# Attention, adapter and feed-forward kernel on one core: GpSimd's indirect transfers tied to TensorE's progress, loads around the hand-over reordered

## The chip, the core and the metric

One core of a Trainium2 chip runs one program. The metric is the device time in microseconds (us) of one execution, lower is better. The profile shows one execution; its span runs from the first to the last instruction.

## The reference

x holds 128 batches of 32 tokens with 512 features, all in float32. What is computed, in order:

- style: every batch picks one of 16 matrices of 32 x 32 by its style id, and its 32 tokens are mixed by it (`einsum('bct,bcd->bdt')`).
- attention on that: q, k, v by w_qkv, clipped to +-8; layer norm of q and k with their weights; 32 heads of 16 features, 32 keys each, bias by distance, causal mask, softmax, output projection; the result is added to x (x1).
- adapter: every batch picks one of 8 matrices of 512 x 512 by its adapter id: y = x1 times that matrix.
- feed-forward on y: relu(y up)^2 down (inner size 1024), plus a routed part, y fc1 expert fc2 scaled per token by the sum of the two largest of 8 gate logits; then layer norm with gamma and beta. Result: x1 plus that.

## The kernel before, in words

The host sorts nothing: the kernel ranks the batches by adapter id itself, makes tables of row numbers, and works on the 4096 tokens as 32 tiles (T) of 128 tokens, 4 batches each, in that order. The large products are exact to nearly float32: each operand is split into a high and a low part, and three products are added (hi x hi, hi x lo, lo x hi). So a projection of one tile is 12 matmuls of 128x128 by 512 columns (L555). ACT makes the high parts, DVE or GpSimd the low ones.

fc1, expert and fc2 are multiplied once at the start: `latent` (L653) and `make_route(c)` (L664, four blocks of four matmuls, c = 0 to 3), copied out of PSUM by ACT (`keep_route`) and stored to HBM by SP's queue.

**Attention** is a software pipeline of 32 rounds, i = 0 to 31, one iteration of a loop written out for each engine. In round i TensorE does, in this order: style of tile i+1 (L545, 8 matmuls); projection of q of tile i; first half of the values of tile i-4 (L573, 48 small matmuls); projection of k; second half of the values; turn_slot (L630); projection of v; the turn of tile i-4's values (L585); the turn of q of tile i-1 (L603); adapt_slot (L644, 12 matmuls); the turn of k; first half of the scores of tile i-2 (L618, 48 small matmuls of 64x32 by 128 columns); the output projection of tile i-4 (L595, 12 matmuls); second half of the scores. ACT scales and rounds q and k, takes the exponential, and copies results out of PSUM; DVE adds bias and takes the row maximum (L1186, L1190), makes low parts, clips, divides, adds x.

GpSimd's round: style_bd for tile i+2 (L1458), scatter_slot of slot i-7 (L1491: rows of y to HBM by an index table), subtract_max of tile i-3 (L1520), low part of the adapter weights (L1526), gather_x and gather_style of tile i+3 (L1470, L1474), low_probs of tile i-3 (L1532), gather_slot of slot i-5 (L1485: rows of x1 back from HBM), the small steps of the layer norm to shift (L1555 to L1565), low part of v (L1569). A slot is up to four batches of one adapter; slots run LAG = 6 rounds behind the tiles. All of these indirect DMAs are issued by GpSimd, which the trace shows busy for about 1 us with each.

The keys and values of four batches are spread into block form (kx, vx) by small copies from SBUF to SBUF on SP's queue (`spread_k` L468, `spread_v` L477, four of 64 or 68 KB each). SP's queue is one list: x1 stores, spreads, weight chunks, y rows (load_y), adapter weights (load_w2, 1 MB each), each behind the waits of what stands before it. In rounds 4 to 23 the feed-forward weights are also split in 20 chunks and the parts stored to HBM; ACT's queue fetches them back later (`fetch`).

**Hand-over.** From round 31 on, the last tiles' attention and the first group's feed-forward are interleaved by hand: turns of y (L681), up(0, f) (L718, 12 matmuls each), scores, values, output projections.

**Feed-forward**: 8 groups of 512 tokens; each has up (8 x 12 matmuls), gates, and four down stages (L735, L742), then normalization on DVE, and a scatter of 128 result rows by GpSimd (`store`, L1498). The remaining slots of the adapter run inside.

The order before, in GpSimd's loop:

```python
                if i > LAG:
                    scatter_slot(i - LAG - 1)
                if live(i - 3):
                    subtract_max(i - 3)
                ...
                if live(i + 3):
                    gather_x(i + 3)
                    gather_style(i + 3)
                if live(i - 3):
                    low_probs(i - 3)
                if i >= LAG - 1:
                    gather_slot(i - LAG + 1)
```

`upto(e, "s", t)` waits until the scores of tile t are done, `upto(e, "o", t)` until its values are; `kx`, `qhi`, `cv` and so on are counted the same way.

## Time and profile before

| | |
|---|---|
| median of 3 runs | 1190.45 us (1190.12 to 1190.9) |
| profiled execution | 1192.36 us, its span 1190.6 us |
| TensorE matmuls | busy 1137.5 us, 96% of the span |
| weight loads (beside the matmuls) | 902.8 us, 76% |
| DVE, ACT, GpSimd | 638.6, 555.7, 705.0 us |
| granted TensorE clock, mean | 0.99 of full speed |
| moved between HBM and core | 98.16 MB read, 38.27 MB written |

PE is TensorE's matmuls, PEld its weight loads, POOL is GpSimd, SP the sync engine; a q behind the name (SPq) is the engine's queue that issues DMAs. A group of instructions shows its start, how long it lasts, the line of the kernel and what it writes and reads; in brackets the idle time of the engine before it and who ended it. "issue" means that the engine waited for nothing that the profile shows. A granted clock of 1.00 is the 2.4 GHz level, 0.50 the 1.2 GHz level.

### The profile page before, as it was taken

How to read it: one execution, taken by the hardware profiler on the slowest of the kernel's cores; microseconds unless marked ns; L12 is line 12 of the kernel's file. 1: busy time of each engine (PE TensorE's matmuls, PEld its weight loads, DVE VectorE, ACT ScalarE, POOL GpSimd, SP SyncE). 2: the span in 40 equal slices, each digit the busy share in tenths (PEclk: the TensorE clock that was granted, in tenths of full speed). 3: DMA queues.
4: the chain of work that ended last, by engine and by line, in shares of the span. 5: the costliest groups of instructions: out<-in, count | busy, mean ns of one | idle time of the engine just before them, and what ended most of it. 6: DMA issues, size and time to landing. Idle time of an engine off the chain costs nothing.

```text
span 1190.6 us, 27392 instructions
## 1 busy us (share of the span) xinstructions
PE 1137.5 (96%) x11124; PEld 902.8 (76%) x11124; DVE 638.6 (54%) x1042; ACT 555.7 (47%) x915; POOL 705.0 (59%) x610
## 2 busy tenths in 40 slices
PE   6999999999999999999997999999999999999994
PEld 4777777777777777777776778787888878787883
DVE  5567575656566666656555344444444444443432
ACT  4365666666666657565655432415142332313120
POOL 4366778787778787878673545545545445433332
PEclk9999999999999999999998999999999999999998
DMA  7124555455554545344455743142413212120101
GB/s 272 45 66 158 176 173 168 170 174 178 154 187 151 193 154 194 118 155 149 142 176 201 251 148 97 62 136 69 137 63 100 82 53 89 54 89 15 56 18 44
DMA packets 60172, 152.38 MB, mean 128 GB/s; under 512 B 11280, under 2 KB 12048, under 8 KB 54672
## 3 DMA queue, kind: packets, MB, share of 16 engines
q1 hardware_dynamic: 42576, 106.06, 26.7%
q0 software_dynamic: 12224, 34.10, 9.0%
q10 hardware_dynamic: 5248, 10.49, 2.5%
q8 instruction: 89, 1.46, 0.5%
q14 instruction: 35, 0.29, 0.1%
HBM read 98.16 MB, written 38.27 MB: 115 GB/s over the span
## 4 chain that ended last, share of the span: by engine, by line
PE 93%; DMA 2%; issue 2%; DVE 1%; ACT 1%; POOL 0%; SPq 0%; ACTq 0%; DVEq 0%
PE bank L555 23%; PE pair L742 15%; PE bank L718 14%; PE bank L644 9%; PE bank L595 8%; PE bank L735 7%; PE pair L618 3%; PE bank L545 3%; PE pair L573 3%; PE bank L603 2%; PE bank L630 2%; PE bank L585 1%; PE bank L691 1%; PE bank L681 1%; DMA kx<-k_hl 1%
## 5 line engine op out<-in xcount | busy, mean ns | idle before, releaser
L1526 POOL TENSOR_TENSOR w_lo<-w2t,w_hi 128x2048 fp32r<-128x2048 f32 x38 | 175.8, 4626 | 13.0 <-ACT w_hi L902 13.0
L555 PE MATMUL bank<-wqkv_hi,h_hi 128*128 128x512 f32 x384 | 159.5, 415 | 3.5 <-ACT q_hi L1000 1.9
L555 PE MATMUL bank<-wqkv_hi,h_lo 128*128 128x512 f32 x384 | 151.5, 395 | 0.5 <-issue 0.5
L555 PE MATMUL bank<-wqkv_lo,h_hi 128*128 128x512 f32 x384 | 150.4, 392 | 0.0
L1578 POOL TENSOR_TENSOR u_lo<-act,u_hi 128x512 fp32r<-128x512 f32 x64 | 82.5, 1290 | 106.5 <-ACT u_hi L1072 106.3
L1613 POOL TENSOR_SCALAR fve<-fmv 128x1 f32<-128x1 f32 x32 | 24.7, 772 | 153.6 <-DVE fmv L1438 153.6
L1520 POOL TENSOR_TENSOR probs<-probs,row_max 128x1024 f32<-128x1024 f32 x32 | 61.1, 1910 | 89.6 <-DVE row_max L1190 89.5
L718 PE MATMUL bank<-yT_hi,up_hi 128*128 128x512 f32 x256 | 103.4, 404 | 0.0
L742 PE MATMUL pair<-down_hi,u_hi 128*128 128x512 f32 x256 | 100.9, 394 | 0.0
L742 PE MATMUL pair<-down_hi,u_lo 128*128 128x512 f32 x256 | 100.8, 394 | 0.0
L718 PE MATMUL bank<-yT_hi,up_lo 128*128 128x512 f32 x256 | 100.6, 393 | 0.0
L718 PE MATMUL bank<-yT_lo,up_hi 128*128 128x512 f32 x256 | 100.3, 392 | 0.0
L742 PE MATMUL pair<-down_lo,u_hi 128*128 128x512 f32 x256 | 100.3, 392 | 0.0
L1383 DVE TENSOR_TENSOR act<-act 128x512 f32<-128x512 f32 x59 | 48.8, 827 | 95.6 <-ACT act L1068 95.6
L555 PEld LDWEIGHTS bank<-wqkv_hi,h_hi 128*128 128x128 f32 x384 | 72.6, 189 | 18.8 <-issue 4.2
L902 ACT ACTIVATE w_hi<-w2t 128x2048 fp32r<-128x2048 f32 x38 | 72.7, 1914 | 30.2 <-DMA w2t<-in_w 30.2
L1433 DVE TENSOR_TENSOR total<-total,pair 128x512 f32<-128x512 f32 x32 | 22.0, 688 | 119.9 <-PE pair L742 119.9
L1068 ACT ACTIVATE act<-bank 128x512 f32<-128x512 f32 x64 | 38.3, 598 | 102.2 <-PE bank L718 102.0
L555 PEld LDWEIGHTS bank<-wqkv_hi,h_lo 128*128 128x128 f32 x384 | 72.5, 189 | 17.7 <-issue 0.9
L1158 ACT ACTIVATE total<-bank,weight 128x512 f32<-128x512 f32 x32 | 22.0, 688 | 131.5 <-PE bank L735 131.5
L555 PEld LDWEIGHTS bank<-wqkv_lo,h_hi 128*128 128x128 f32 x384 | 72.7, 189 | 13.7 <-issue 0.8
L1532 POOL TENSOR_TENSOR p_lo<-probsT,p_hi 128x1024 bf16<-128x1024 f32 x32 | 69.1, 2158 | 23.3 <-ACT p_hi L945 22.8
(175 smaller groups left out, 2915.8 us busy)
## 6 DMA issues: line engine op xcount, KB each, us to landing
w2t<-in_w SPq DMA_DIRECT2D x38, 1024.0 KB
vx<-v_hl SPq DMA_DIRECT2D x128, 68.0 KB
x_rows<-x1t SPq DMA_DIRECT2D x32, 256.0 KB, 4.6
x1g<-x_rows SPq DMA_DIRECT2D x32, 256.0 KB, 3.4
kx<-k_hl SPq DMA_DIRECT2D x124, 64.0 KB
yt<-y_rows SPq DMA_DIRECT2D x7, 1024.0 KB, 6.7
ffn_high<-w_high SPq DMA_DIRECT2D x20, 256.0 KB, 4.2
ffn_low<-w_low SPq DMA_DIRECT2D x20, 256.0 KB, 4.5
```

Of the source, the lines that this page charges most:

```text
L555: m = e.matmul(into, a[:, c, :], b[:, n, c, :], start=(c == 0 and k == 0), stop=(c == KC - 1 and k == 2))
L595: m = e.matmul(B6, a[:, j, :], b[:, j, :], start=(j == 0 and k == 0), stop=(j == BPT - 1 and k == 2))
L644: m = e.matmul(into, a[:, P * c:P * c + P], b[:, c, :], start=(c == 0 and k == 0), stop=(c == KC - 1 and k == 2))
L718: i = e.matmul((B2, B3)[n % 2], a[:, w, cols], b[m % 2][:, c, :], start=(c == 0 and k == 0), stop=(c == KC - 1 and k == 2))
L735: i = e.matmul((B6, B7)[n % 2], a[m % 2][:, c, toks], b[:, c, :], start=(c == 0 and k == 0), stop=(c == KC - 1 and k == 2))
L742: i = e.matmul(pair[:, n % 2, :], a[f][:, toks], b[:, f, :], start=(f == 0 and k == 0), stop=(f == FC - 1 and k == 2))
L902: e.activation(w2_hi[:, :, :], w2t[:, :, :], ACT.Copy).then_inc(d_whi, 1)
L1383: e.tensor_tensor(act[n % 2][:, :], act[n % 2][:, :], act[n % 2][:, :], ALU.mult) \
L1520: e.tensor_tensor(probs[:, :, :], probs[:, :, :], row_max[:, :].rearrange("p (h o) -> p h o", o=1) .broadcast_to([P, HEADS, SEQ]), ALU.sub ...
L1526: e.tensor_tensor(w2_lo[:, :, :], w2t[:, :, :], w2_hi[:, :, :].bitcast(F32), ALU.subtract).then_inc(d_wlo, 1)
L1532: e.tensor_tensor(p_lo[:, :], probsT[:, :], p_hi[:, :], ALU.subtract).then_inc(A["plo"], 1)
L1578: e.tensor_tensor(u_lo[n % FC][:, :], act[n % 2][:, :], u_hi[n % FC][:, :].bitcast(F32), ALU.subtract) \
```

## The change

- GpSimd: scatter_slot waits for the scores of tile i-3 (for the last slot, tile T-3); gather_x and gather_style wait for the values of tile i-4; gather_slot stands ahead of low_probs. In the start the style rows of tile 0 are gathered before its x rows, with semaphores of their own, and gather_x(1) comes behind the first style. In the down stages the store of the tile before is issued ahead of the wait for the statistics.
- Start: the ids are the first loads of SP's queue; the second part of the constants is loaded by ACT's queue. Only make_route(0) stays ahead of round 0; make_route(1), (2), (3), their copies and stores move to rounds 2, 3, 4 (and one round later for the stores), into another bank.
- Keys of tiles 0 to 2 are turned in bank B4 instead of B5, without the wait for DVE's clip of v; ACT rounds q and k of tile 0 at the end of round 1 instead of at the start of round 2.
- Hand-over: the up weights are fetched in two sets, the even chunks (2 MB) in round 31 where all (4 MB) were, the odd ones (2 MB) after high_probs(T-3); up(0,4) waits for those. y of group 1 and the adapter weights of slot_up(0) are loaded behind the v spread of tile T-2 and the x1 store of T-4; the last v spread moves ahead of the x1 store of tile T-3.

```diff
--- before
+++ after
@@ -323,6 +323,7 @@
     a_x = [sem(f"a_load{i}") for i in range(XR)]
+    a_rows = [sem(f"a_rows{i}") for i in range(XR)]
     a_store = [sem(f"a_store{i}") for i in range(2)]
@@ -349,7 +350,8 @@
     m_gate, m_ghi, m_glo = sem("m_gate"), sem("m_ghi"), sem("m_glo")
-    m_up, m_route, m_down = sem("m_up"), sem("m_route"), sem("m_down")
+    m_up = [sem("m_up_low"), sem("m_up_high")]
+    m_route, m_down = sem("m_route"), sem("m_down")
     d_zero, d_w2, d_x = sem("d_zero"), sem("d_w2"), [sem("d_x0"), sem("d_x1")]
@@ -380,6 +382,12 @@
+    def k_bank(t):
+        return B4 if t < 3 else B5
+
+    def route_bank(c):
+        return pair[:, 0, :] if c == 0 else B6
+
     def last_slot(m):
@@ -388,7 +396,6 @@
-            e.dma_start(cst[:, C_WMASK:C_SIZE], consts[:, C_WMASK:C_SIZE]).then_inc(s_cst, 16)
             for dst, src in ((ids_row[:, :], adapter_ids.broadcast_to([P, BATCHES])),
@@ -401,17 +408,18 @@
             load_stage(1)
-            e.wait_ge(a_x[0], 32)
+            e.wait_ge(a_x[0], 16)
             load_stage(2)
...
             load_stage(3)
-            for c in range(KC):
+            def store_route(c):
                 e.wait_ge(s_routec, c + 1)
                 e.dma_start(route_rows[:, c, :], route_f[c][:, :]).then_inc(s_kept, 16)
+
+            store_route(0)
             e.dma_start(gate_raw[:, :, :], gate).then_inc(m_gate, 16)
             e.wait_ge(s_tables, 2)
-            e.wait_ge(s_route, KC)
@@ -488,15 +496,15 @@
                     spread_k(i - 2)
+                if i in (3, 4, 5):
+                    store_route(i - 2)
                 if 0 <= i - 4 < CHUNKS:
...
                     load_y(0)
-                if i == T - 1:
-                    load_y(1)
-                if i >= LAG - 1:
+                if LAG - 1 <= i < T - 1:
                     load_w2(i - LAG + 1)
@@ -507,8 +515,10 @@
             store_x1(T - 4)
+            load_w2(slot_up(0))
+            load_y(1)
+            spread_v(T - 1)
             store_x1(T - 3)
-            spread_v(T - 1)
@@ -536,7 +546,7 @@
-                e.wait_ge(a_x[t % XR], 32 * (t // XR + 1))
+                e.wait_ge(a_x[t % XR], 16 * (t // XR + 1))
                 upto(e, "style", t)
@@ -588,7 +598,9 @@
                 upto(e, "olo", t)
-                e.wait_ge(s_wlo, 4)
+                if t == 0:
+                    e.wait_ge(s_wlo, 4)
+                    e.wait_ge(s_routec, KC)
                 upto(e, "x1", t - 1)
@@ -659,9 +671,9 @@
                 if c >= 2:
-                    e.wait_ge(s_routec, c - 1)
+                    e.wait_ge(s_routec, c)
                 for k in range(LC):
-                    m = e.matmul(pair[:, c % 2, :], latT[:, k, P * c:P * c + P], fc2_sb[:, k, :],
+                    m = e.matmul(route_bank(c), latT[:, k, P * c:P * c + P], fc2_sb[:, k, :],
                                  start=(k == 0), stop=(k == LC - 1))
@@ -704,9 +716,11 @@
                 if n == 0:
-                    e.wait_ge(m_up, 64)
+                    e.wait_ge(m_up[0], 64)
                     upto(e, "khi", T - 1)
                     upto(e, "klo", T - 1)
+                if n == KC:
+                    e.wait_ge(m_up[1], 32)
                 if n >= 2:
@@ -753,7 +767,6 @@
             e.matmul(B4[:, 0:1], after[:, :], first[:, :], start=True, stop=True).then_inc(s_tp, 1)
-            make_route(0)
             style(0)
@@ -761,7 +774,7 @@
                 .then_inc(s_tp, 1)
-            make_route(1)
+            make_route(0)
             for i in range(T):
@@ -773,8 +786,9 @@
                 if i == 0:
-                    make_route(2)
                     style(1)
+                if i in (2, 3, 4):
+                    make_route(i - 1)
                 if live(i - 4):
@@ -782,8 +796,6 @@
                     project(i, 1, B3, "pk")
-                if i == 0:
-                    make_route(3)
                 if live(i - 4):
@@ -803,8 +815,9 @@
                 if live(i - 1):
-                    upto(e, "cv", i)
-                    turn_qk(i - 1, kn[(i - 1) % 2], "kn", B5, "tk")
+                    if i > 3:
+                        upto(e, "cv", i)
+                    turn_qk(i - 1, kn[(i - 1) % 2], "kn", k_bank(i - 1), "tk")
                 if live(i - 2):
@@ -920,6 +933,12 @@
+            def fetch_up(ready, part, first_, last_):
+
+                dst = (up_hi, up_lo)[part][:, first_:last_:2, :]
+                e.dma_start(dst.bitcast(F32), ffn_parts[part][first_:last_:2].rearrange("c p n -> p c n")) \
+                    .then_inc(ready, 16)
+
             def high_y(m, c):
@@ -968,16 +987,16 @@
                 e.wait_ge(s_route, c + 1)
-                e.activation(route_f[c][:, :], pair[:, c % 2, :], ACT.Copy).then_inc(s_routec, 1)
-
+                e.activation(route_f[c][:, :], route_bank(c), ACT.Copy).then_inc(s_routec, 1)
+
+            e.dma_start(cst[:, C_WMASK:C_SIZE], consts[:, C_WMASK:C_SIZE]).then_inc(s_cst, 16)
             high_weights(0)
...
                 keep_lat(n)
+            high_h(0)
             high_weights(1)
             keep_route(0)
-            high_h(0)
             high_weights(2)
-            keep_route(1)
             e.wait_ge(s_qkln, 16)
@@ -1010,16 +1029,15 @@
                 live = lambda t: 0 <= t < T
-                if live(i - 2):
+                if i >= 3:
                     high_q(i - 2, B3)
-                    high_k(i - 2, B5, k_hl)
-                if i == 0:
-                    keep_route(2)
+                    high_k(i - 2, k_bank(i - 2), k_hl)
                 if live(i + 1):
...
                     high_weights(3)
-                    keep_route(3)
+                if i in (2, 3, 4):
+                    keep_route(i - 1)
                 if i == 2:
@@ -1030,16 +1048,16 @@
                     upto(e, "pq", T - 1)
-                    fetch(m_up, up_hi[:, 0:4, :], 0, 0, 4)
-                    fetch(m_up, up_lo[:, 0:4, :], 1, 0, 4)
+                    fetch_up(m_up[0], 0, 0, 4)
+                    fetch_up(m_up[0], 1, 0, 4)
                 if live(i - 3):
...
                     upto(e, "pk", T - 1)
-                    fetch(m_up, up_hi[:, 4:8, :], 0, 4, 4)
-                    fetch(m_up, up_lo[:, 4:8, :], 1, 4, 4)
+                    fetch_up(m_up[0], 0, 4, 8)
+                    fetch_up(m_up[0], 1, 4, 8)
                 if live(i - 4):
@@ -1050,7 +1068,10 @@
                     scale_q(i - 1, B3)
-                    scale_k(i - 1, B5)
+                    scale_k(i - 1, k_bank(i - 1))
+                if i == 1:
+                    high_q(0, B3)
+                    high_k(0, k_bank(0), k_hl)
                 if i >= LAG:
@@ -1088,6 +1109,8 @@
             high_probs(T - 3)
+            fetch_up(m_up[1], 0, 1, 8)
+            fetch_up(m_up[1], 1, 1, 8)
             relu(0)
@@ -1336,7 +1359,7 @@
                     low_q(i - 2, B3)
-                    low_k(i - 2, B5, k_hl)
+                    low_k(i - 2, k_bank(i - 2), k_hl)
                 upto(e, "pq", t)
@@ -1454,7 +1477,7 @@
                 upto(e, "h", t - 2)
-                e.wait_ge(a_x[t % XR], 32 * (t // XR + 1))
+                e.wait_ge(a_rows[t % XR], 16 * (t // XR + 1))
                 e.tensor_tensor(style_bd[t % 2][:, :, :],
@@ -1472,7 +1495,7 @@
                 e.indirect_dma_start(out=style_rows[t % XR][:, :], out_offset=None, in_=style_w,
-                                     in_offset=rows(style_idx, t)).then_inc(a_x[t % XR], 16)
+                                     in_offset=rows(style_idx, t)).then_inc(a_rows[t % XR], 16)
@@ -1506,11 +1529,11 @@
             e.wait_ge(s_tables, 1)
+            gather_style(0)
             gather_x(0)
-            gather_style(0)
-            gather_x(1)
             e.wait_ge(s_cst, 16)
             style(0)
+            gather_x(1)
             gather_style(1)
@@ -1537,6 +1560,7 @@
                 if i > LAG:
+                    upto(e, "s", i - 3)
                     scatter_slot(i - LAG - 1)
@@ -1545,12 +1569,13 @@
                 if live(i + 3):
+                    upto(e, "o", i - 4)
                     gather_x(i + 3)
                     gather_style(i + 3)
+                if i >= LAG - 1:
+                    gather_slot(i - LAG + 1)
                 if live(i - 3):
                     low_probs(i - 3)
-                if i >= LAG - 1:
-                    gather_slot(i - LAG + 1)
                 upto(e, "aggr", t)
@@ -1578,6 +1603,7 @@
+            upto(e, "s", T - 3)
             scatter_slot(LAST)
@@ -1609,14 +1635,14 @@
                     n = GROUP * m + t
+                    if n:
+                        store(n - 1)
                     e.wait_ge(S["aggr"], n + 1)
...
                         .then_inc(S["rstd"], 1)
-                    if n:
-                        store(n - 1)
                     if t == 1:
...
                             scatter_slot(slot_down(m))
```

## Rows read from the trace of the kernel before

**Rows 1.** The page, part 4: the chain that ended last, by engine.
```profile
PE 93%; DMA 2%; issue 2%; DVE 1%; ACT 1%; POOL 0%; SPq 0%; ACTq 0%; DVEq 0%
```

**Rows 2.** TensorE's waits: us in total, times, longest us.
```profile
PE pair L618 <- issue: 10.2, 30, 0.5
...
PE pair L618 <- DMA kx<-k_hl: 5.3, 1, 5.3
...
PE bank L555 <- ACT q_hi L1000: 1.9, 1, 1.9
...
PE bank L644 <- DVE xgT_lo L1179: 1.5, 1, 1.5
PE bank L603 <- DVE vf L1168: 1.0, 3, 0.3
```

**Rows 3.** Windows over 54 score halves: from:to length, busy and count by engine.
```profile
127.04:128.41 1.37, 0.86 (x48) 0.60 (x48) 1.00 0.91 298
...
446.68:447.21 0.53, 0.53 (x48) 0.46 (x48) 1.00 0.12 39
...
sum 48.68, PE 37.99 PEld 28.36; mean PE 0.70 PEld 0.53
```

**Rows 4.** One round: start us, us, engine, line, operation [idle before <-releaser].
```profile
429.27 0.47 POOL L1458 TENSOR_TENSOR style_bd<-style_rows,cst 128x128 f32<-128x128 f32 x1
...
429.91 1.10 POOL L1491 DMA_INDIRECT y_rows<-ys,slot_rows  x1 [0.17 <-issue]
...
430.63 0.68 DVE L1220 TENSOR_TENSOR x1t<-bank,xt 128x512 f32<-128x512 f32 x1
...
431.19 0.25 PE L618 MATMUL pair<-kx,q_hi 64*32 64x128 bf16 x4 [0.29 <-issue]
...
434.14 1.91 POOL L1520 TENSOR_TENSOR probs<-probs,row_max 128x1024 f32<-128x1024 f32 x1 [3.13 <-DVE row_max L1190]
...
439.26 0.66 PE L630 MATMUL bank<-cst,xg 128*128 128x128 f32 x4
...
440.79 1.01 POOL L1470 DMA_INDIRECT xt<-in_x,tile_rows  x1 [0.16 <-issue]
...
445.39 1.03 POOL L1485 DMA_INDIRECT xg<-x_rows,slot_rows  x1 [0.16 <-issue]
```

**Rows 5.** Windows over values halves (two together, one clean), timeline at 78.
```profile
sum 2.98, PE 1.76 PEld 1.20; mean PE 0.88 PEld 0.60
...
111.42:111.98 0.56, 0.56 (x48) 0.45 (x48) 1.00 0.02 7
...
78.04 0.39 PE L555 MATMUL bank<-wqkv_hi,h_hi 128*128 128x512 f32 x1 [0.49 <-issue]
```

**Rows 6.** Timeline of the start; window with its granted clock (0.50).
```profile
18.92 1.98 PE L664 MATMUL pair<-fc_sb,latT 128*128 128x512 f32 x4
...
27.04 0.46 POOL L1458 TENSOR_TENSOR style_bd<-style_rows,cst 128x128 f32<-128x128 f32 x1 [3.78 <-DMA style_rows<-in_style_w,style_idx]
...
50.56:53.97 3.41, 3.41 (x9) 2.65 (x8) 0.61 (x2) 0.00 (x0) 0.00 (x0) 0.50 0.23 81
```

**Rows 7.** The hand-over: window (clock, DMA share, GB/s last), timeline, page part 6.
```profile
628.00:634.00 6.00, 4.04 (x125) 3.59 (x120) 5.05 (x8) 4.57 (x11) 1.90 (x1) 1.00 1.05 405
...
633.49 0.22 PE L573 MATMUL pair<-vx,p_lo 128*32 128x68 bf16 x4 [1.68 <-issue]
...
636.61 1.25 DVE L1224 TENSOR_TENSOR yT_lo<-bank,yT_hi 128x512 fp32r<-128x512 f32 x2
...
641.22 0.77 PE L718 MATMUL bank<-yT_hi,up_hi 128*128 128x512 f32 x1
...
x1g<-x_rows SPq DMA_DIRECT2D x32, 256.0 KB, 3.4
```

**Rows 8.** Timeline of the end.
```profile
1178.49 0.75 DVE L1447 SCALAR_TENSOR_TENSOR ot<-total,frstd,x1g 128x512 f32<-128x512 f32 x1 [0.94 <-POOL frstd L1616]
1179.88 0.96 POOL L1498 DMA_INDIRECT out<-ot,tile_rows  x1 [0.30 <-issue]
```

## The prediction, made before the changed kernel ran

> **What bounds the kernel now.** I read the page's chain first: TensorE carries 93% of it [rows 1]. So no other engine has to get faster; what can be won is time in which TensorE stands. Next come the waits of TensorE, longest in total first [rows 2]. The largest is no wait for a result: 10.2 us before score matmuls, in 30 pieces of at most 0.5 us, put down to "issue". Then 5.3 us once, for a copy into kx; 1.9 us once, for q_hi; 1.0 us in three waits for DVE's clip of v. The adapter's matmuls (L644, 456 of them) have one wait, for DVE, and none on issue.
>
> The third reading is of single score halves: 48 small matmuls each, from their first matmul to the first of the next group [rows 3]. A clean half takes 0.53 us, the one at 127.04 took 1.37. From round 5 to round 31 there are 54 halves with 48.68 us in all, so 48.68 - 54 x 0.53 = 20.1 us are lost in them; 20 of the 54 are clean. The fourth is the timeline of one round [rows 4]. GpSimd issues its scatter from 429.91 to 431.01; the second score half began at 430.33, issued 44 of its 48 matmuls, stood for half a microsecond and finished with four at 431.19. In the round after, the slot gather runs from 445.39 to 446.42 and the first half starts at 446.68: clean. Where that gather comes 0.3 us later, the first half is hit too. Each of the 34 slow halves has an indirect DMA of GpSimd over it, none of the 20 clean ones has. Two halves of values in rounds 4 and 5 lie under gathers as well: 2.98 us for both, where a clean one takes 0.56 (row of 111.42) [rows 5].
>
> **Scatter and slot gather (the main term).** Scatter s now waits for the scores of that round's end, so its 1.10 us start behind them, at some 431.0 instead of 429.91, under style's eight matmuls and the first project. It costs GpSimd nothing: it idles 3.13 us before subtract_max [rows 4], which waits for the row maximum, itself later than the scores; 1.1 us of scatter fit. What is queued behind it (subtract_max, low_w2) keeps its time. The gathers wait for values of four tiles back, over at 439.26 in that round; GpSimd reaches gather_x only at 440.79 [rows 4], 1.5 us later, so this wait never ends last in the steady rounds. The slot gather goes ahead of low_probs: 443.2 to 444.2, 2.4 us before the scores; low_probs shifts by 1.1 us to 446.4, and values need it 9 us later. The instructions behind them (var_eps to shift) stay. GpSimd's round then ends with style_bd at 429.74, 1.1 us before the earlier end of the scores. In rounds with a weight chunk DVE's add of x ends only at 431.31 [rows 4], so the maximum moves forward by 0.1 of the 0.5 us; the project that needs the low part of q, made after it, still starts 0.8 us behind it, so TensorE is not held. I take the whole 20.1 us; the low end is 7, where each of the 26 scatters costs a 0.5 us stall in its new place.
>
> **Values in rounds 4 and 5.** 2.98 - 2 x 0.56 = **1.9 us**; gathers wait until values are over. Low_probs comes up to 2 us later, needed a round later.
>
> **Start.** Ids go first and the other constants by ACT's queue: SP spends some 0.47 us on each issue, so ids leave and land 0.45 us earlier. Four route blocks of 1.9 to 2.0 us each (18.92 is one; back to back 1.4 to 1.8 us) [rows 6] stood ahead of and between the first projects; one stays, three move to rounds 2, 3 and 4. That frees 5.0 us at the start. But tile 2's style rows, issued by 20.60, landed only just before 27.04 (GpSimd waited 3.78 us for them) [rows 6]: the weight loads share the transfer. So data cap what TensorE can gain. Tile 1's rows are now asked for 0.5 us later, behind GpSimd's first style_bd; by tile 2's delay I put their landing near 23.3 us. With style, project of k and project of v from there, round 1 starts 2.9 us earlier (ends: 0, if the landings rule, and 5.0). The three blocks cost 5.0 again in rounds 2 to 4. What they fill: the 1.9 us wait for q_hi, which also goes because ACT rounds q of tile 0 before it waits for the statistics, and 0.8 us before project in round 3 (low part of q). With the 1.9 us wait goes what followed it: from 50.56 to 53.97 the granted clock was 0.50, the 1.2 GHz level [rows 6], 3.4 us for 1.7 us of work. Turning k into bank 4 for the first three tiles drops the 1.0 us on DVE's v [rows 2]. Start: 2.9 - 5.0 + 1.9 + 1.7 + 0.8 + 1.0 = **3.3 us**, ends 0.4 and 5.4.
>
> **Hand-over from attention (round 31 on).** Here TensorE stood 1.68 us inside values and 5.30 us until kx landed [rows 7]; the DMA engines were full (share 1.05, 405 GB/s) with four 1 MB loads of up weights, 1 MB of y and 1 MB of adapter weights. Two of the four, y and the adapter now go behind the spreads. SP's queue reaches the k spread at 628.6 as before, its four issues end at 631.0, and by the 3.4 us from issue to landing that the median load of x1g takes [rows 7], an upper bound for a copy a quarter as large, kx is there by 634.4. That doesn't give 6 us: up(0,0) needs the low parts of all four turned y chunks, and DVE made the last at 636.61 to 637.86, behind a transpose that waits for ACT's exp, a chain from the scores at 628 with no DMA in it. Up(0,0) started at 641.22 and can start at 637.7: **3.5 us**. What is late next is that low part. The clock had fallen to the 1.2 GHz level (0.77 us for the matmul at 641.22, where the one at 78.04 took 0.39) [rows 5, 7]; TensorE will still stand some 1 to 2.4 us at two places here, so I count nothing back; the high end, clock held and y chunks a little earlier, is 6. The low end is -2: the odd up weights (2 MB) with y and adapter weights (2 MB) collide with the last v spreads. Against it: a low transfer between 645 and 660, and the first odd chunk is needed for up(0,4), over 20 us after its issue. Scatters behind the last spread and x1 stores keep their place relative to TensorE. As to the 1.68 us: the Trainium skill (Runtime: NRT & Kernel Launch, Instruction fetch mechanics) has TensorE's instructions fetched ahead, in 16 KiB blocks by a DMA queue of its own, mostly hidden; by it, that pause would be no matter of full DMA engines and would stay. The sum would fall by 0.2 us only, since values would then end at 633.5 and the y chain still rule. The trace can't say which it is.
>
> **End.** The last but one store now goes before the last tile's statistics instead of behind them. It held the last store: ot was done at 1179.24, its store issued at 1179.88 [rows 8]. **0.5 us.** In the other down stages nothing waits for stores.
>
> **Sum:** 20.1 + 1.9 + 3.3 + 3.5 + 0.5 = **29.3 us**. The profiled execution took 1192.36 us (span 1190.6): 1163.1. The median of the runs is 1.9 us below the profiled one, so 1161.2 us. Ends: 7 + 0 + 0.4 - 2 + 0 = 5 us and 20.1 + 1.9 + 5.4 + 6 + 0.5 = 34 us.
>
> **Rivals.**
> The stall moves. The scatter now begins 0.1 us behind 48 small matmuls that have emptied what was issued ahead. In round 4, project behind a values half stood 0.49 us at 78.04, a gather having just ended [rows 5]. If style is hit so, 26 x 0.5 = 13 us come back: 1174 us. Against: there the gather had already stopped the issue before the block was through; with the whole score block issued, style and the first project want 40 instructions in 3.8 us. On this the Trainium skill (Advanced Engine Details and Errata, Engine Queue Depths) gives TensorE a queue of 64 instructions; 44 matmuls with their weight loads, 88, got out before the stall [rows 4], so the trace shows a somewhat deeper one. By a strict 64, style could start on a shorter queue than I assume, which is this rival's 1174. Chance 0.09.
> The stalls are the score halves' own (instruction stream), not GpSimd's. Then 20.1 stay: 1181 us. Against: the 20 clean halves. 0.04.
> Slower: every indirect DMA stops TensorE's issue wherever it lands, and three now come in a row (440.8 to 444.2), so what was issued ahead doesn't last over them. At 0.5 us for each of four, 26 rounds cost 52 us, less the 29: 1213 us. It decides from 1.1 us of new stall a round. Against: L644 shows no issue wait, though gathers lay over 26 of its 38 blocks [rows 2]. 0.04.
> Start and hand-over give nothing or cost (data landings rule): 1168 to 1171 us. It lies in my range. 0.08.
>
> **Numbers.** Forecast 0.75, its own range 1156 to 1168. With the rival at 1174 the range is 1155 to 1175. Within 0.2% (2.4 us, about what a measurement can tell here): 0.01; slower 0.04; faster 0.95.
>
> **What would show it.** All score halves of rounds 5 to 31 at 0.53 us and no issue wait there; rounds of 19.3 us instead of 19.8 to 20.8; scatters starting within 0.3 us behind the scores; style still 0.9 us. No wait for q_hi and full clock from 45 to 60 us. Up(0,0) some 3.5 us nearer to the last scores, its wait on DVE's y low part. I am wrong if style or project take on issue waits, if GpSimd's shift comes behind ACT's need, or if up(0,4) waits for DMA.

## The result and the profile after

The changed kernel takes **1163.87 us** (median of 4 runs, 1163.0 to 1164.47), the kernel before 1190.28 us beside it (4 runs, 1188.94 to 1190.9): a ratio of 0.9779, 95% interval 0.9762 to 0.9796. The profiled execution took 1163.74 us, its span is 1162.0 us; the one before had 1190.6 us. The 28.6 us between the spans can be laid out along TensorE's blocks, by the starts of the first style block of round 6, the end of the scores of round 31, up(0,0) and the last matmul:

| stretch | before | after | gained |
|---|---|---|---|
| start to round 6 | 107.58 us | 101.62 us | 6.0 |
| round 6 to the end of round 31's scores | 520.40 | 501.85 | 18.5 |
| from there to up(0,0) | 13.24 | 9.54 | 3.7 |
| up(0,0) to the last matmul | 533.81 | 533.55 | 0.3 |
| last matmul to the end of the span | 15.55 | 15.41 | 0.1 |

(The medians differ by 26.4 us only: the profiled execution of before, 1192.36 us, stood 2.1 us above the 1190.28, that of the changed kernel at its median.)

The same 54 score halves as in [rows 3], in windows over the changed kernel; the columns are length, busy and count of PE and PEld, granted clock, DMA share, GB/s:

```profile
426.46:426.99 0.53, 0.53 (x48) 0.46 (x48) 1.00 0.00 0
...
487.98:488.56 0.58, 0.58 (x48) 0.47 (x48) 1.00 1.07 452
...
sum 30.22, PE 30.10 PEld 24.93; mean PE 0.56 PEld 0.46
```

48.68 us have become 30.22, 18.5 less, and no half is longer than 0.62. First halves (as at 426.46) take 0.53 to 0.57, second halves (as at 487.98) 0.57 to 0.62, all but the last one. One round in the timeline of the changed kernel, to be laid beside [rows 4]:

```profile
429.20 0.47 POOL L1481 TENSOR_TENSOR style_bd<-style_rows,cst 128x128 f32<-128x128 f32 x1
...
430.30 0.28 PE L630 MATMUL pair<-kx,q_hi 64*32 64x128 bf16 x8
...
430.56 1.13 PE L555 MATMUL bank<-style_bd,xt 128*128 128x128 f32 x8
...
431.43 1.11 POOL L1514 DMA_INDIRECT y_rows<-ys,slot_rows  x1 [1.75 <-PE pair L630]
433.51 1.91 POOL L1543 TENSOR_TENSOR probs<-probs,row_max 128x1024 f32<-128x1024 f32 x1 [0.97 <-DVE row_max L1213]
...
442.74 1.03 POOL L1508 DMA_INDIRECT xg<-x_rows,slot_rows  x1 [0.30 <-issue]
```

GpSimd now waits 1.75 us for the scores, then scatters over style and project, from 0.87 us behind the half's end on (0.83 to 0.90 in the 26 rounds); it still has 0.97 us to spare ahead of the row maximum. Style's blocks take 0.88 us as before, and adapter blocks 2.84: nothing has moved there. TensorE's waits in the changed kernel from 25 us on (which wait, us in total, times, longest):

```profile
PE pair L630 <- DVE on L1234: 2.4, 1, 2.4
PE bank L703 <- DVE yT_lo L1247: 1.7, 1, 1.7
PE pair L583 <- POOL p_lo L1555: 1.5, 1, 1.5
PE bank L615 <- DVE kn L1191: 1.1, 1, 1.1
PE bank L656 <- DVE xgT_lo L1202: 0.9, 1, 0.9
PE bank L732 <- DVE yT_lo L1247: 0.7, 1, 0.7
```

Of [rows 2], the issue waits before scores, the wait for kx, the one for q_hi and those for v are gone. New are the one for kn, in round 1, and in the hand-over those for `on` (2.4 us) and for yT_lo ahead of up(0,0) (0.7). The hand-over in the timeline of the changed kernel, beside [rows 7]:

```profile
607.06 0.35 PE L583 MATMUL pair<-vx,p_hi 128*32 128x68 bf16 x4
...
608.91 0.76 DVE L1234 TENSOR_TENSOR on<-pair,recip 128x256 f32<-128x256 f32 x2
...
609.82 0.31 PE L630 MATMUL pair<-kx,q_hi 64*32 64x128 bf16 x8 [2.41 <-DVE on L1234]
...
611.71 1.25 DVE L1247 TENSOR_TENSOR yT_lo<-bank,yT_hi 128x512 fp32r<-128x512 f32 x2
...
613.01 0.79 PE L732 MATMUL bank<-yT_hi,up_hi 128*128 128x512 f32 x1 [0.67 <-DVE yT_lo L1247]
```

Values run through without a pause. The scores wait for `on` (the divide frees their bank), up(0,0) for the low part of y. The first up matmul still takes 0.79 us: the granted clock was at the 1.2 GHz level from 609.3 to 616.1, where before it had been from 634.2 to 644.5.

### The profile page after: what moved, and what is told of

It is laid out like the page before. It is cut to its first block, busy times and chain, and to the rows that moved or that the text cites. A ratio compares the mean times of both kernels' runs of the same rounds, so it can differ in the third digit from the quotient of the medians.

```text
span 1162.0 us, 27444 instructions
## 1 busy us (share of the span) xinstructions
PE 1127.1 (97%) x11124; PEld 898.3 (77%) x11124; DVE 657.0 (57%) x1042; ACT 552.3 (48%) x915; POOL 708.4 (61%) x610
## 3 DMA queue, kind: packets, MB, share of 16 engines
q8 instruction: 89, 1.46, 0.6%
## 4 chain that ended last, share of the span: by engine, by line
PE 93%; DVE 2%; issue 2%; DMA 1%; POOL 1%; ACT 0%; SPq 0%; DVEq 0%; ACTq 0%
PE bank L565 22%; PE pair L756 15%; PE bank L732 15%; PE bank L656 9%; PE bank L607 8%; PE bank L749 8%; PE pair L630 3%; PE bank L555 3%; PE pair L583 3%; PE bank L615 2%; PE bank L642 2%; PE bank L703 1%; PE bank L595 1%; PE bank L693 1%; DMA x_rows<-x1t 1%
```

## The experiments

e1 to e4 ran beside each other, e5 to e8 in a second comparison, e9 to e12 in a third, each on another chip and with its own runs of the kernel before. The changed kernel itself was in none of the three: where a time is set against its 1163.87 us, the two come from different comparisons.

**e1_scatter_wait_off: the changed kernel without the wait ahead of the scatters.**

```diff
-                    upto(e, "s", i - 3)
                     scatter_slot(i - LAG - 1)
...
-            upto(e, "s", T - 3)
             scatter_slot(LAST)
```

> The changed kernel without the two waits of the scatters for the scores. Theory (an indirect DMA that GpSimd issues while the 48 small matmuls of a half run holds back TensorE's issue): the scatters lie over the second score halves again, those halves go from 0.58 to about 1.1 us, 26 of them, so 13 to 14 us come back: 1177 us. The first halves stay at 0.53. Rival (the stalls belong to the score halves and went for another reason): no change, 1164 us. Rival (the scatter costs the same wherever it lies): no change in the sum, 1164 us, with shorter style and project blocks.

Measured: 1178.69 us (before: 1189.69), ratio 0.9917 (0.9893 to 0.9942). Its timeline, in one second half, and then the row of its windows for that half and the sum over the 54:

```profile
418.97 1.10 POOL L1514 DMA_INDIRECT y_rows<-ys,slot_rows  x1 [0.18 <-issue]
...
419.57 0.26 PE L630 MATMUL pair<-kx,q_hi 64*32 64x128 bf16 x5
...
420.25 0.24 PE L630 MATMUL pair<-kx,q_hi 64*32 64x128 bf16 x3 [0.42 <-issue]
```

```profile
419.25:420.46 1.21, 0.79 (x48) 0.54 (x48) 1.00 0.91 366
...
sum 43.84, PE 35.11 PEld 26.97; mean PE 0.65 PEld 0.50
```

Taking the wait away brings back 13.6 us of halves (43.84 - 30.22) and 14.8 us of time. In this half 45 matmuls get out and three wait until the scatter is over. The 24 halves with a scatter over them take 0.83 to 1.24 us (median 1.2), none of the other 30 takes over 0.60.

**e2_gpsimd_only: the kernel before with GpSimd's part alone** (both waits, the slot gather ahead of low_probs).

```diff
+                    upto(e, "s", i - 3)
                     scatter_slot(i - LAG - 1)
...
+                    upto(e, "o", i - 4)
                     gather_x(i + 3)
                     gather_style(i + 3)
+                if i >= LAG - 1:
+                    gather_slot(i - LAG + 1)
                 if live(i - 3):
                     low_probs(i - 3)
```

> The kernel before with only GpSimd's steady order changed: scatters wait for the scores, gathers for the values, the slot gather ahead of low_probs. Theory: the whole steady term, 18.5 us from the score halves and 1.6 us from the values halves of rounds 4 and 5, comes from these few lines: 1170 us. Rival (the rounds are also shorter because the route blocks and the start were moved, so that GpSimd is elsewhere): less than 15 us, above 1175 us.

Measured: 1170.21 us, ratio 0.9843 (0.9818 to 0.9867): 19.5 of the 26 us. The halves have 30.36 us. Round 6 begins at 105.04 us, 2.5 earlier than before and 3.4 later than in the changed kernel. The start's own part is worth those 3.4 and perhaps some of the clock's: this kernel has the same wait for q_hi as before, but the granted clock stays at the 2.4 GHz level behind it, where before it fell [rows 6]. Its timeline, and a window of it:

```profile
50.62 0.47 PE L555 MATMUL bank<-wqkv_hi,h_hi 128*128 128x512 f32 x1 [1.90 <-ACT q_hi L1000]
```

```profile
50.56:53.97 3.41, 3.35 (x15) 2.82 (x16) 1.98 (x4) 0.22 (x2) 0.28 (x1) 1.00 0.33 121
```

The wait for kx (5.0 us) and a pause inside values (2.3 us) are still there.

**e3_handover_only: the kernel before with the hand-over alone** (even up weights in round 31, odd ones after it; adapter weights and y of group 1 behind the last spread of k).

```diff
                 if i == T - 1:
-                    load_y(1)
...
-                if i >= LAG - 1:
+                if LAG - 1 <= i < T - 1:
                     load_w2(i - LAG + 1)
...
             store_x1(T - 4)
-            store_x1(T - 3)
+            load_w2(slot_up(0))
+            load_y(1)
             spread_v(T - 1)
+            store_x1(T - 3)
...
```

> The kernel before with only the hand-over changed: up weights in two sets, y of group 1 and adapter weights behind the spreads. Theory: 3.5 to 4 us, from the last scores of round 31 to the first up block 9.5 us instead of 13.2: 1186.5 us; the 1.68 us pause inside values goes too. Rival (the instruction fetch is not touched by full DMA engines): the pause of about 1.7 us stays. Rival (loads pushed back cost later): 1190 us, with waits for DMA before up(0,4) or adapt.

Measured: 1187.26 us, ratio 0.998 (0.9965 to 0.9995), 2.4 us faster (0.6 to 4.2). From the last scores to up(0,0) it takes 9.55 us, as in the changed kernel; the halves keep their stalls. The scores wait 2.4 us for `on`, as there.

**e4_direct_scatter: e1 with another form of scatter.** A plain DMA of GpSimd writes each ys to fixed rows, so the rows of y stand in other places than the reference's; everything else is e1.

```diff
-                e.indirect_dma_start(out=y_rows, out_offset=rows(slot_rows, s), in_=ys[s % 2][:, :],
...
+                e.dma_start(y_rows[first_row:first_row + P, :], ys[s % 2][:, :]).then_inc(d_y[s % 2], 16)
```

> As the first run (no wait for the scores), but the scatter of y rows is a plain DMA of the same size to fixed rows, still issued by GpSimd; y rows are then in the wrong places, the work is the same. It tells whether the index table or GpSimd's issuing itself stops TensorE. If the indirect form is the cause: the second halves stay at 0.53 to 0.6, 1164 us. If any DMA that GpSimd issues does it: 1170 to 1177 us, by how long GpSimd is busy with the plain one. I lean to the second, 60 to 40.

Measured: 1164.7 us, ratio 0.9795 (0.9771 to 0.982). I leaned the other way and was wrong. Its timeline, the window of that half and the sum over the 54:

```profile
410.77 0.67 POOL L1515 DMA_DIRECT2D y_rows<-ys  x1
```

```profile
411.00:411.59 0.59, 0.59 (x48) 0.46 (x48) 1.00 0.98 403
...
sum 30.24, PE 30.07 PEld 24.93; mean PE 0.56 PEld 0.46
```

That half has more traffic beside it (403 GB/s) than e1's at 419.25 (366 GB/s) and is clean, so full DMA engines alone don't make the stall. The plain DMA also lies over the half, but ends 0.44 us behind its start; the indirect ones end later. So compare at equal ends: on the same chip indirect DMAs that ended 0.48 and 0.49 us behind the half's start made it 0.83 and 0.88 us long, plain ones with 0.44 to 0.49 left it at 0.57 to 0.67. Over before, e1, e3 and e5 the length of a hit half is the end of the indirect DMA plus 0.32 to 0.54 us, 0.39 in the median of 97 halves: 0.18 gave 0.67, 0.39 gave 0.88, 0.95 gave 1.32, 1.13 gave 1.57. The plain ones don't follow that; none of them ended later than 0.5 us, but for one that began only at 0.50 and left a half of 0.62.

**e5_slot_gather_late: the changed kernel with the slot gather behind low_probs again.**

```diff
-                if i >= LAG - 1:
-                    gather_slot(i - LAG + 1)
                 if live(i - 3):
                     low_probs(i - 3)
+                if i >= LAG - 1:
+                    gather_slot(i - LAG + 1)
```

> The changed kernel with only the slot gather put back behind low_probs. In the changed kernel's trace the gather would then end, in the rounds from tile 6 on, between 0.2 us behind and level with the first matmul of the first score half. My theory (a half is hit only by so much as the indirect DMA outlasts the 44 matmuls that get out, about 0.5 us from the half's start): first halves stay under 0.8 us, at most 0.2 us lost in each of some 20, so 0 to 4 us: 1164 to 1168, no issue wait before scores of more than 1 us in total. Rival (any overlap of an indirect DMA with a half costs a full 0.5 us): 20 halves of 1.0 us or more, 10 us, 1174. Second rival (the place of the slot gather doesn't matter at all): 1164 with halves of 0.53 to 0.56.

Measured: 1170.29 us (before: 1190.19), ratio 0.9828 (0.9806 to 0.9849). Neither my number nor the rival's: 48 of the 54 halves are clean and six are hit, five of them hard. Windows:

```profile
352.24:353.91 1.67, 0.95 (x48) 0.56 (x48) 1.00 0.42 64
...
430.79:431.32 0.53, 0.53 (x48) 0.46 (x48) 1.00 0.00 0
...
sum 35.16, PE 31.97 PEld 25.64; mean PE 0.59 PEld 0.47
```

At 430.79 the gather had ended 0.02 us behind the first matmul, at 352.24 it began 0.19 us behind it. The halves explain 4.9 of the 6.4 us. Of the rest 0.8 us is up(0,0), which lay longer under the lower clock (5.06 us instead of 4.28), and 0.2 us lie ahead of round 6; for some 0.5 I have no row. By the halves, the place of the slot gather is worth about a third of what the scatter's is (4.9 to 13.6 us).

**e6_up_weights_at_once: the changed kernel with all 4 MB of up weights fetched in round 31.**

```diff
                     fetch_up(m_up[0], 1, 4, 8)
+                    fetch_up(m_up[1], 0, 1, 8)
+                    fetch_up(m_up[1], 1, 1, 8)
...
             high_probs(T - 3)
-            fetch_up(m_up[1], 0, 1, 8)
-            fetch_up(m_up[1], 1, 1, 8)
```

> The changed kernel with all up weights (4 MB) fetched in round 31 again, y of group 1 and the adapter weights still behind the last spreads. My theory: the four spreads of k of tile 30 land as now, and TensorE's wait ahead of the last scores stays DVE's (2.4 us), since the SP queue's place and not the amount of data made the 5.3 us: 1164, up(0,0) within 0.5 us of now, 9.5 us behind the last scores. Rival (the amount of data in flight delays the spreads and stops TensorE inside values): the pause of 1.7 us inside values comes back and the kx wait too; but up(0,0) hangs on DVE's y low part, so the time would rise by 0 to 2 us: 1164 to 1166. The trace tells them apart by the pause and by the releaser of the wait.

Measured: 1164.41 us, ratio 0.9785 (0.9768 to 0.9802). The timeline:

```profile
608.42 0.22 PE L583 MATMUL pair<-vx,p_lo 128*32 128x68 bf16 x4 [0.61 <-issue]
...
610.41 0.31 PE L630 MATMUL pair<-kx,q_hi 64*32 64x128 bf16 x8 [1.74 <-DVE on L1234]
```

The pause inside values is back, 0.61 us of it, and what follows waits that much less for `on`: nothing is lost. Splitting the up weights was not needed for the time; moving y and the adapter weights behind the spreads was what freed kx. Whether by their place in SP's queue or by the 2 MB less in flight, no run separates.

The view of the DMA queues shows what goes with the pauses. Queue q8 carries instructions: 89 packets with 1.46 MB, 16 KB each, and each of the two below takes 1.1 to 1.2 us. The packet that falls into the hand-over, by the quarter of a microsecond in which it moves: before, in 631.00 to 631.25,

```profile
q8 instruction: 1, 0.02, 27.7%
```

and in the changed kernel, in 603.75 to 604.00:

```profile
q8 instruction: 1, 0.02, 28.9%
```

| kernel | start of the packet behind the end of round 31's scores | pause inside values |
|---|---|---|
| changed | 0.5 us | none |
| e3 | 1.1 | none |
| e6 | 1.8 | 0.6 us |
| before | 3.1 | 1.7 |
| e11 | 3.3 | 2.0 |
| e2 | 3.6 | 2.3 |

The pause is the packet's delay less 1.2 to 1.4 us, and in all four kernels that have one it ends 1.2 to 1.4 us behind the packet's last byte. So TensorE had most likely run out of instructions, and the next 16 KB came late while the DMA engines were full (share 1.05 [rows 7]). This is read from the traces of six kernels, some of which differ in their loads; no run changes the packet alone. The Trainium skill (Runtime: NRT & Kernel Launch, Instruction fetch mechanics) has the instructions fetched ahead in blocks of 16 KiB by a queue of their own, "mostly hidden"; queue and block size agree with these rows, and the fetch is hidden in the changed kernel, but not under 400 GB/s.

**e7_divide_first: another order of DVE in the hand-over of the changed kernel.**

```diff
             bias_max(T - 3)
+            divide(T - 4)
             low_k(T - 1, B2, k_last)
             low_y(0, 0)
-            divide(T - 4)
             low_y(0, 1)
-            turn_probs(T - 3)
             low_y(0, 2)
             low_y(0, 3)
+            turn_probs(T - 3)
```

> The changed kernel with DVE's order in the hand-over changed: the divide of tile 28 right behind the row maximum, then the low part of k, the four low parts of y, and only then the transpose of the probabilities. Theory (TensorE there waits for nothing but DVE): the scores of tile 30 start 1.1 us earlier (wait 2.4 to 1.3 us) and up(0,0) 1.1 us earlier at 611.9 in the trace's time; the transpose comes 1.3 us later, and 4 us of slack of values behind p_lo cover it. If the clock then doesn't fall, 1.4 us more from up(0,0). 1160.5 to 1163. Rival (the transpose is needed: values wait for p_lo in its place): 1164 to 1165, with a wait of values for POOL p_lo longer by 1 us.

Measured: 1162.08 us (1161.54 to 1163.26), ratio 0.977 (0.9754 to 0.9787); the changed kernel wasn't in that comparison, e6 and e8 there have 1164.41 and 1163.97. The timeline:

```profile
609.59 0.25 PE L630 MATMUL pair<-kx,q_hi 64*32 64x128 bf16 x8 [1.42 <-DVE on L1234]
...
612.49 0.50 PE L732 MATMUL bank<-yT_hi,up_hi 128*128 128x512 f32 x1 [1.14 <-DVE yT_lo L1247]
```

From the last scores (604.24) to up(0,0) it takes 8.25 us instead of 9.54, 1.3 less where 1.1 were expected, and in this execution the clock stays at the 2.4 GHz level, so that up(0,0) takes 2.84 us instead of 4.28. The wait of values for p_lo stays at 1.3 us (1.5 in the changed kernel): the transpose can come later.

**e8_start_more: two edits at the start of the changed kernel.**

```diff
-                e.memset(vx[:, :, :, :, :], 0.0).then_inc(A["zero"], 1)
+                e.memset(vx_flat[:, :].bitcast(F32), 0.0).then_inc(A["zero"], 1)
...
             gather_x(0)
+            gather_style(1)
             e.wait_ge(s_cst, 16)
             style(0)
             gather_x(1)
-            gather_style(1)
```

> The changed kernel with two edits at the start: the 3.7 us memset of vx on DVE is written as half as many 4-byte elements, and the style rows of tile 1 are gathered ahead of GpSimd's wait for the constants and its first style_bd. Theory: the memset takes 1.8 to 1.9 us (kx's of 2048 4-byte elements takes 1.76), and the wait of turn_qk for kn (1.13 us) is gone; style(1) starts up to 1.0 us earlier, where its rows land before 22.7. Together -1.1 to -2.1 us: 1162. Rival (landings are set by the weight loads that share the transfer, not by the time of issue): style(1) stays, -1.1 us. Second rival (the gained time turns into a wait for the next DVE or GpSimd result): 0, 1164.

Measured: 1163.97 us, ratio 0.9779 (0.976 to 0.9797): no gain. GpSimd's and DVE's rows of the timeline:

```profile
14.45 1.92 POOL L1498 DMA_INDIRECT style_rows<-in_style_w,style_idx  x1 [0.30 <-issue]
16.48 0.47 POOL L1482 TENSOR_TENSOR style_bd<-style_rows,cst 128x128 f32<-128x128 f32 x1
...
34.93 1.87 DVE L1337 MEMSET vx<- 128x2176 f32 x1 [0.40 <-issue]
```

The memset is halved and the wait for kn is gone; round 2 begins at 40.47 instead of 41.46. The gather took twice its usual time and held the first style block by 0.6 us (17.10 for 16.52). At the last scores 0.7 us of the gain are left, and then the clock takes them: it falls for as long as in the changed kernel, but over more of up(0,0), which takes 0.75 us longer. So in time the gain isn't shown and isn't refuted: the one of the four executions with a mean clock of 0.995 took 1161.72 us, the three with 0.992 took 1163.85 to 1164.49.

**e9_two_plain_scatters: e4 with the plain DMA cut in two**, so that GpSimd issues through the whole half. As in e4, the rows of y stand in other places.

```diff
-                e.indirect_dma_start(out=y_rows, out_offset=rows(slot_rows, s), in_=ys[s % 2][:, :],
...
+                for half in (0, 64):
+                    e.dma_start(y_rows[first_row + half:first_row + half + 64, :], ys[s % 2][half:half + 64, :]) \
+                        .then_inc(d_y[s % 2], 16)
```

> The kernel of e4_direct_scatter (no wait ahead of the scatter, plain DMA of GpSimd to fixed rows; y rows stand in the wrong places) with the DMA cut in two of 64 rows, one behind the other. In e4 the one plain DMA ended 0.25 to 0.5 us behind the half's first matmul, and the half took 0.57 to 0.6 us; the indirect ones of four kernels follow half = end of the DMA + 0.38 us from an end of 0.18 on (0.39 gave 0.88, 0.68 gave 1.03 to 1.11, 0.95 gave 1.32). Here the second DMA should end some 1.0 us behind the half's start. My theory (only the indirect form stops TensorE's issue): halves stay at 0.53 to 0.7 us, total of the 56 halves under 34 us, 1164 to 1166. Rival (e4 was clean only because the plain DMA ended early): halves of 1.3 us in some 24 rounds, total near 50 us, 1180 or more.

Measured: 1167.45 us, and the kernel before in this third comparison took **1171.69 us** (16 runs, 1170.17 to 1173.26), 18 us less than in the other two. The halves have 30.23 us, with second DMAs that end 0.83 to 1.08 us behind the start of halves of 0.57 to 0.61. But this can't decide between the two forms, for the reason that e11 shows: on this chip the indirect form doesn't stall either. Of the 3 us more than e4, 2.3 lie behind the last matmul: GpSimd's closing DRAIN takes 9.88 us, in the changed kernel 7.58. Why is open.

**e10_ids_and_stores_back: two small parts undone.**

```diff
+            e.dma_start(cst[:, C_WMASK:C_SIZE], consts[:, C_WMASK:C_SIZE]).then_inc(s_cst, 16)
             for dst, src in ((ids_row[:, :], adapter_ids.broadcast_to([P, BATCHES])),
...
-            e.dma_start(cst[:, C_WMASK:C_SIZE], consts[:, C_WMASK:C_SIZE]).then_inc(s_cst, 16)
             high_weights(0)
...
-                    if n:
-                        store(n - 1)
                     e.wait_ge(S["aggr"], n + 1)
...
+                    if n:
+                        store(n - 1)
```

> The changed kernel with two small parts undone: the other constants are loaded first on SP's queue again, ahead of the ids, and in the down stages the store stands behind the statistics again. Theory from the trace: the ids' order gave nothing (style_col landed at 6.82 us in both kernels), the last store began 0.29 us behind ot in the changed kernel and 0.64 in the one before, so +0.2 to +0.4 us: 1164.1, within the measurement. Rival, the prediction's own terms (0.45 for the ids, 0.5 for the end): +0.9, 1164.8. The trace tells: the landing of style_col, the start of the last store behind ot.

Measured: 1164.6 us (before there: 1171.69), ratio 0.994 (0.9925 to 0.9956). The landing of style_col is at 6.73 us with the constants first, 6.82 with the ids first: the order does nothing. The last store begins 0.64 us behind ot instead of 0.29, and the stretch behind the last matmul is 15.63 us instead of 15.41.

**e11_start_only: the kernel before with the start's part alone** (ids first, the first gathers, the route blocks, q of tile 0, k_bank; all as in the change's diff).

```diff
-            gather_x(0)
             gather_style(0)
-            gather_x(1)
+            gather_x(0)
             e.wait_ge(s_cst, 16)
             style(0)
+            gather_x(1)
...
+                if i in (2, 3, 4):
+                    make_route(i - 1)
```

> The kernel before with the start's part of the change alone (ids first, three route blocks moved to rounds 2, 3 and 4, gathers and q of tile 0 in the new order, k turned into bank 4 for three tiles); GpSimd's scatters and gathers, the hand-over and the stores as before. Theory (the parts add up; in the changed kernel round 6 began 6.0 us earlier, and 3.4 us earlier than with GpSimd's part alone): round 6 begins 3.0 to 3.6 us earlier than before, 1186.7. Rival (the start gains only together with clean halves, since the waits moved): round 6 under 2 us earlier, 1188.5 or more.

Measured: 1168.87 us, ratio 0.9976 (0.9967 to 0.9985) to the 1171.69 beside it, so 2.8 us for the start (1.8 to 3.9). The number I had expected was of the other chips, and the rival isn't tested, since the halves are clean here anyway; what its trace shows of GpSimd is the finding. Timeline and windows:

```profile
430.70 1.11 POOL L1503 DMA_INDIRECT y_rows<-ys,slot_rows  x1 [0.18 <-issue]
...
431.20 0.34 PE L629 MATMUL pair<-kx,q_hi 64*32 64x128 bf16 x8
```

```profile
430.88:431.51 0.63, 0.63 (x48) 0.52 (x48) 1.00 1.14 416
...
sum 30.99, PE 30.82 PEld 25.61; mean PE 0.57 PEld 0.47
```

This kernel has neither the waits nor the new order, and indirect DMAs lie over its halves as before. One that ended 0.93 us behind the first matmul left a half of 0.63, where e3 on another chip has 1.34 for 0.93. The 54 halves have 30.99 us, hardly more than in the changed kernel. The kx wait (4.5 us) and the pause in values (2.0 us) are there as elsewhere. There is no trace of the kernel before on this chip, and each chip was in one comparison only: that the chip makes the difference is the nearest reading, not a shown one.

**e12_divide_and_memset: e7 with e8's memset, without e8's gather.**

```diff
-                e.memset(vx[:, :, :, :, :], 0.0).then_inc(A["zero"], 1)
+                e.memset(vx_flat[:, :].bitcast(F32), 0.0).then_inc(A["zero"], 1)
...
             bias_max(T - 3)
+            divide(T - 4)
             low_k(T - 1, B2, k_last)
...
-            divide(T - 4)
             low_y(0, 1)
-            turn_probs(T - 3)
...
             low_y(0, 3)
+            turn_probs(T - 3)
```

> The changed kernel with DVE's hand-over order of e7 and the memset of vx in 4-byte elements of e8, but GpSimd's gathers at the start in the changed kernel's order (in e8 the gather of tile 1's style rows ahead of style_bd took 1.92 us and held the first style block by 1.3 us). Theory: 1.0 us from the memset (turn_qk no longer waits for kn), 1.3 us from the order; 1.4 us more if the clock holds through up(0,0), as it did in e7. 1161 with the clock held, 1162.4 without. Rival (e7's gain was the clock's chance alone, and the gained 1.0 us turns into a wait for the rows of tile 2): 1163 to 1164.

Measured: **1160.68 us** (5 runs, 1160.1 to 1162.65), ratio 0.9912 (0.9898 to 0.9925) to the kernel before beside it, 3.9 us below e10 in the same comparison. The wait for kn is gone, up(0,0) comes 8.16 us behind the scores, and in the profiled execution the clock stays up. It is the fastest kernel of this case. Four of its five executions have a mean clock of 0.993 to 0.995 and took 1160.1 to 1161.52 us, the fifth 0.992 and 1162.65, so what the clock gives is not certain in every execution.

## Why the prediction was right, and where it was not

The forecast was 1161.2 us, the kernel takes 1163.87, in the likeliest case's own range; against the profiled execution 29.3 us were predicted and 28.6 came. Of the 2.7 us between forecast and time, 0.7 lie in the terms and 2.0 in the step from the profiled execution to the median: I took off 1.9 us because the kernel before's profiled execution was so much above its median, and the changed kernel's (1163.74) was not.

- **Scatter and slot gather**, 20.1 predicted, 18.5 measured. The mechanism as forecast: e2 gives it alone, e1 and e5 undo its halves. The size was off because 0.53 us is the first half's length; second halves take 0.57 to 0.62 even when clean (30.22 us for 54, not 28.6). Beside 26 of the 27 the DMA engines are full (share 0.95 to 1.10); but the first half at 542.39 has 1.12 beside it and takes 0.53, so the reason stays open. None of the rivals' new stalls came: style stayed at 0.88 us. The scatter begins 0.83 to 0.90 us behind the scores, not the 0.1 to 0.3 that I wrote, so one that follows within 0.3 us was not tested. The 44 matmuls that got out in [rows 4] are no fixed number either: in before, e1 and e3 it was 37 to 45, mostly 43 to 45, so no depth of a queue can be read from them.
- **Values in rounds 4 and 5**, 1.9 predicted; those four halves went from 4.31 to 2.45 us, 1.9 less, and all 56 halves of values from 32.3 to 30.7, 1.6 less.
- **Start**, 3.3 predicted; of the 6.0 us by which round 6 comes earlier, 3.9 are left without the halves of values and of scores. Against e2 it is 3.4, and e11 gives 2.8 us. That the sum fits is partly luck, since inside it three terms were wrong. The ids bring nothing (I took 0.45 us from the issue time, but DVE starts at 6.91 us, before at 6.92; the landing rules). And a step was left out: the memset of vx on DVE, 3.7 us, stood behind the last wait and now holds turn_qk by 1.1 us. The landing of tile 1's rows was right (style_bd at 23.16, put near 23.3), round 1 gained 3.2 for 2.9, and the three blocks cost 4.8 for 5.0. The third is the clock's 1.7 us, which I tied to the wait for q_hi: it stayed at the 2.4 GHz level from 50 to 54 us as forecast, but it did so in e2 too, behind the same wait of 1.90 us. So the wait alone doesn't bring it down, and its going doesn't explain the clock.
- **Hand-over**, 3.5 predicted, 3.7 measured, the same in e3's trace (its medians give 2.4, 0.6 to 4.2). "What is late next is that low part" is right for up(0,0), but the wait ahead of the scores, 2.4 us, is DVE's divide, which stands behind the low parts of k and y; e7 takes 1.0 us of it away and brings up(0,0) 1.3 us nearer. The pause inside values: I set the Trainium skill's rule (Runtime: NRT & Kernel Launch, Instruction fetch mechanics) against full DMA engines as if one excluded the other. By the packets of q8 the two go together: fetched ahead and hidden, but not beside 400 GB/s.
- **End**, 0.5 predicted. The store came 0.35 us sooner behind ot, but took 1.09 us instead of 0.96; 0.1 to 0.2 us reached the end of the span. The 0.5 was the gap between ot and the store, and 0.29 of it stays.
- What the prediction could not know: that the largest term is not there on every chip. The comparisons of e1 and e5 ran on two chips that show it; on the third the kernel before has 1171.69 us, the changed one without its two small parts 1164.6, a gain of 7 us made of start, hand-over and under 1 us of halves. The prediction had no case for that: it took 20 of its 29 us from a loss that the trace of one chip showed, and that the result came from a chip with that loss was luck.

Left open: why the indirect form stops TensorE's issue on some chips, and whether the plain form is free of it through a whole half there. Both would need a chip that stalls.

## What to carry to other kernels

When TensorE shows short issue waits in one kind of block only, lay GpSimd's indirect DMAs over the blocks and sort them into hit and clean ones; if they part, move the DMA by a wait under large matmuls, where it cost nothing here. Measure such a gain on more than one chip before counting on it. After a transfer wait is removed, read DVE's order next: the instruction that frees TensorE's bank belongs first.

## What the runs showed of the hardware

- An indirect DMA of GpSimd (1.0 to 1.1 us) over 48 small matmuls stopped their issue after 37 to 45 of them, until 0.1 to 0.3 us past its end: 0.1 to 1.1 us a half on two chips, at most 0.2 us on a third. Over blocks of 128x512 matmuls no issue wait was seen, but for the 0.49 us at 78.04 behind a half that was hit itself [rows 5].
- Instruction packets of 16 KB share the DMA engines: beside some 400 GB/s one started 3.1 to 3.6 us behind the scores instead of 0.5, and TensorE stood 1.7 to 2.3 us.
- The granted clock in the hand-over: waits of 2.4 and 0.7 us ahead of the scores and of up(0,0), and it fell to the 1.2 GHz level for 7 us; the same 2.4 us with 1.5 us in e1, and it stayed at 2.4 GHz, but with 1.6 us in e9 it fell. In e7 and e12, with 1.4 and 1.1 us, it stayed. Up(0,0) took 2.87 us in e1 and 5.29 in e9. What the clock costs here, 1.4 us in the changed kernel, is not fully in the kernel's hand.
- DVE's memset of the same bytes took 3.69 us in 2-byte and 1.87 us in 4-byte elements.
